# First pass of a graph network kernel: one 384-column scalar-tensor-tensor per dense step in place of three 128-column tensor-scalars in every second step

## Chip, cores and metric

The kernel runs on one core of one Trainium2 chip. The metric is the device time of one execution in microseconds (us), lower is better. Before the change it is 4443.65 us, the median of three runs (4441.05 to 4446.47).

## The reference, cut to what matters

Four graph layers run one after the other on 3125 nodes with 64 features and 50,000 edges (`src`, `dst`, sorted by `dst`). Each layer gathers rows of the source nodes, makes messages and sums them per destination node.

```python
h = jnp.maximum(_layernorm(x), 0.0)
x = x + L0(h, edge_index, edge_attr_16, ...)   # msg = relu(h[src] + edge_attr @ We + be); segment_sum over dst; MLP
x = x + L1(h, edge_weight, src, dst)           # 10 steps: h = 0.9 * segment_sum(h[s] * wn, d) + 0.1 * h0
x = x + L2(h, edge_index, edge_attr_3, ...)    # 3 attention layers over the edges
x = x + L3(h, edge_index, ...)                 # edge convolution, segment_sum over src
```

L1 applies the same weighted adjacency matrix ten times. The kernel therefore builds that matrix once, dense, while it computes L0, and L1 is then a series of plain matrix products.

## The kernel before, in words

Edges are sorted into 416 tiles of 128 (`T`). A pass over the edges handles them in 104 units of `K` = 4 tiles, as 13 iterations (`NB`) of 8 units (`U`). There are five such passes; the change touches the first one, which does L0 and builds the dense matrix at the same time.

Every engine runs its own instruction list, written out by hand, and the lists meet at semaphores. In the first pass one unit is this:

- **GpSimd** (`gather`, L825) issues four indirect DMAs, one per tile, that fetch the rows of the source nodes from the table in HBM into `rows[:, u]`. It may run up to eight units ahead, held by `slots_free`; in each unit it also waits once until the unit before has landed.
- **VectorE** (`turn0` of the vector block) first makes the four one-hots of the *next* unit (`one_hots`: L1169 copies the weights, L1174 makes four 128x128 one-hots). Then `dense_operands` makes the operands of 5 or 6 dense steps (44 in an iteration, 572 in all). Then it copies the transposed payload of the next unit (L1201) and, after `lin_ready`, takes the relu of this unit's messages (L1217).
- **TensorE** transposes the next payload (L1672), makes the messages from payload and gathered rows (it waits for `gathered[u]` there), sums up the unit two before, and then runs the unit's dense steps: three matmuls of 500 columns per step.
- **ScalarE** (`evict`, L1447 and L1449) copies each finished block of the matrix out of PSUM and clears the bank.

A dense step needs two operands. `lhs[:, slot]` holds three weighted one-hots of 128 columns in bf16, one for each of the three bf16 parts into which a float32 weight is split (its largest part, what is left of it, and what is left then). `rhs[:, slot]` is a one-hot of 500 columns (L1158). The operands lie in a ring of `PER2` = 11 slots; `built` says when TensorE has used a slot, `op_ready` when a slot is filled.

Before the change the three weighted one-hots are made in two ways, in turns. An even step uses three tensor-scalars of 128 columns (L1156), each with two per-partition scalars (the edge's row and its weight part from `w_left`). An odd step uses one scalar-tensor-tensor of 384 columns (L1150), whose inputs are the row of column numbers, repeated three times, and the three weight parts from `w_parts`, each repeated 128 times. Both of these inputs lie in SBUF.

Of the kernel before, what the change touches and what calls it, by code (L numbers as in the profile page):

```python
# [25 lines left out]
ALU = mybir.AluOpType  # L26
# [69 lines left out]
def gnn_kernel(nc, x, src, dst, edge_attr_16, edge_attr_3, edge_weight,  # L96
# [3 lines left out]
    with ExitStack() as ctx:  # L100
        def sb(name, shape, dt=F32):
            return ctx.enter_context(nc.sbuf_tensor(name, shape, dt))
# [18 lines left out]
        iota_row_b = sb("iota_row_b", [128, 128], BF16)  # L121
# [72 lines left out]
        def carve(shape, dt=F32):  # L194

            n = 1
            for d in shape[1:]:
                n *= d
            w = -(-n // 2) if dt in (BF16, F16) else n
            assert used[0] + w <= WORDS, (used[0], w)  # L200
            a = arena[0:shape[0], used[0]:used[0] + w]
            used[0] += w
            if dt != F32:
                a = a.bitcast(dt)[:, 0:n]
            if len(shape) > 2:
                names = "abcd"[:len(shape) - 1]
                a = a.rearrange(f"p ({' '.join(names)}) -> p {' '.join(names)}",
                                **{x: d for x, d in zip(names, shape[1:])})
            return a
# [93 lines left out]
        lhs = carve([128, PER2, 3, 128], BF16)  # L303
# [4 lines left out]
        lo_col = carve([128, T])  # L308
        src_blk = carve([128, T])
        src_all = carve([128, T])  # L310
        w_left = carve([128, 3, T])
        w_parts = carve([128, T, 3], BF16)
# [251 lines left out]
        def first_step(u):  # L564

            return u // 2 * PER2 + u % 2 * PER_U[0]
# [275 lines left out]
        def _(v):  # L842
# [299 lines left out]
            def dense_operands(i, u):  # L1142

                first = first_step(u)
                for k in range(PER_U[u % 2]):
                    slot = (first + k) % PER2
                    tile_at, key_at = operand_at["tile", first + k], operand_at["key", first + k]
                    v.wait_ge(built, i * PER_BODY + (first + k + 1))
                    if (first + k) % 2:
                        nc.vector.scalar_tensor_tensor(  # L1150
                            lhs[:, slot], iota_row_b[:].unsqueeze(1).to_broadcast([128, 3, 128]), lo_col[:, bass.ds(tile_at, 1)],
                            w_parts[:, bass.ds(tile_at, 1), :].rearrange("p o c -> p (o c)").unsqueeze(2).to_broadcast([128, 3, 128]),
                            ALU.is_equal, ALU.mult)
                    else:
                        for part in range(3):
                            nc.vector.tensor_scalar(lhs[:, slot, part, :], iota_row_b[:], lo_col[:, bass.ds(tile_at, 1)],  # L1156
                                                    w_left[:, part, bass.ds(tile_at, 1)], ALU.is_equal, ALU.mult)
                    nc.vector.tensor_scalar(rhs[:, slot, :], iota_col_h[:], flat_keys[:, bass.ds(key_at, 1)], None,  # L1158
                                            ALU.is_equal).then_inc(op_ready, 1)

# [42 lines left out]
            def turn0(i, u, before, more):  # L1203
                if u == 0:
                    fetch_operands(i, u)
                if before == 0:
                    one_hots(i, u, pay, C_KEY, True, False)
                    turn_keys(i, u)
                if more:
                    one_hots(i, u + 1, pay, C_KEY, True, False)  # L1210
                dense_operands(i, u)
                if u + 1 < U:
                    fetch_operands(i, u + 1)
                if more:
                    turn_keys(i, u + 1)
                v.wait_ge(lin_ready, i * U + (u + 1))
                nc.vector.tensor_scalar(of(msg, u)[:, :, 0:D], lin(u), 0.0, None, ALU.max).then_inc(msg_ready, 1)  # L1217
# [693 lines left out]
```

## Time and profile before

| | |
|---|---|
| median of 3 runs | 4443.65 us |
| profiled execution | 4435.5 us |
| its span, first to last instruction | 4433.7 us |
| TensorE busy | 3310.6 us (75%) |
| VectorE busy | 2910.4 us (66%) |
| GpSimd busy | 3018.6 us (68%) |
| ScalarE busy | 847.9 us (19%) |
| first pass, first gather to its last matmul | about 657.7 to 1345.8 us |

How to read it: times are microseconds from the start of the span, of one execution taken by the hardware profiler. PE is TensorE, PEld its weight load, DVE is VectorE, ACT is ScalarE, POOL is GpSimd. L1156 is line 1156 of the kernel. Instructions of one engine overlap a little at their ends, so the cost of one among others is read from start to start, not from its own duration.

### The profile page before, as it was taken

What the parts mean: (1) busy time and instruction counts of PE and PEld (TensorE: products, weight loads), DVE (VectorE), ACT (ScalarE), POOL (GpSimd) and SP (SyncE); (2) the same over time, 40 slices, a digit from 0 to 9 for tenths busy, and PEclk for the clock granted to TensorE, in tenths of its full rate; (3) what the DMA queues carried; (4) which work ended last, traced back from release to release, by engine and by line L of the source; (5) the groups of instructions that cost most, each with busy time, mean ns of one, the idle gap of its engine ahead of it and who ended that gap; (6) DMA issues with size and microseconds to landing.
All of it is one profiled execution on the core that took longest, in us unless ns stands there. A gap on an engine that the chain in (4) does not pass through costs nothing.

```text
span 4433.7 us, 80945 instructions
## 1 busy us (share of the span) xinstructions
PE 3310.6 (75%) x20757; PEld 2267.7 (51%) x20758; DVE 2910.4 (66%) x10438; ACT 847.9 (19%) x2207; POOL 3018.6 (68%) x3059
## 2 busy tenths in 40 slices
PE   1269408888887999999687876888858877566666
PEld 1269304554553444443466665666646666445554
DVE  6987319999993111111788887888878888765554
ACT  0000002222221000000122222222212222121121
POOL 2677767788778888840377774777747777467776
PEclk9999999999997999999899996999979999755555
DMA  4310013333458999999222223222232222211112
GB/s 143 108 46 10 17 59 81 88 90 90 92 88 314 356 363 356 363 357 361 80 62 62 61 62 51 63 62 62 62 52 63 62 62 62 33 32 28 28 28 30
DMA packets 295276, 497.76 MB, mean 112 GB/s; under 512 B 165611, under 2 KB 210540, under 8 KB 293674
## 3 DMA queue, kind: packets, MB, share of 16 engines
q1 hardware_dynamic: 120119, 340.02, 21.7%
q0 software_dynamic: 92160, 115.39, 13.6%
q10 hardware_dynamic: 82800, 40.01, 3.1%
q8 instruction: 88, 1.44, 0.1%
q14 instruction: 109, 0.89, 0.1%
HBM read 435.66 MB, written 59.08 MB: 112 GB/s over the span
## 4 chain that ended last, share of the span: by engine, by line
PE 29%; POOL 24%; issue 18%; DMA 16%; DVE 9%; DVEq 1%; SPq 1%; ACT 1%; POOLq 0%; ACTq 0%
PE ps L1565 27%; POOL arena L825 17%; DMA arena<-table,arena 13%; POOL rows_dst L808 7%; DMA rows_dst<-stage,arena 2%; PE ps L1754 1%; DMA arena<-in_edge_attr_dram 1%; DVE arena L1174 1%; DVE arena L1173 1%; DVE arena L1156 1%; DVEq L553 1%; DVE arena L1158 1%; DVE arena L1192 1%; DVE arena L1150 1%; DMA arena<-dense 1%
## 5 line engine op out<-in xcount | busy, mean ns | idle before, releaser
L825 POOL DMA_INDIRECT arena<-table,arena x2080 | 2110.2, 1015 | 1046.5 <-issue 541.3
L1565 PE MATMUL ps<-arena 125*128 (+5 forms) x9976 | 1629.7, 339 | 580.5 <-DVE arena L1192 250.9
L1565 PEld LDWEIGHTS ps<-arena 125*128 125x128 bf16 (+5 forms) x9976 | 1187.8, 206 | 990.8 <-issue 606.5
L1565 PE MATMUL ps<-arena,nodes 125*64 125x500 f32 (+2 forms) x3144 | 651.4, 537 | 34.6 <-DMA arena<-dense 24.1
L1174 DVE TENSOR_SCALAR arena<-iota_row_b,arena 128x128 f32<-128x128 bf16 x2080 | 584.9, 299 | 0.0
L808 POOL DMA_INDIRECT rows_dst<-stage,arena x400 | 401.0, 1002 | 233.0 <-issue 122.2
L779 POOL DMA_INDIRECT rows_src<-stage,stage_at x400 | 479.0, 1197 | 116.4 <-issue 108.4
L1186 DVE TENSOR_TENSOR arena<-ps,arena 128x256 f32<-128x256 f32 x416 | 176.6, 425 | 523.9 <-DMA arena<-table,arena 510.4
L1173 DVE TENSOR_SCALAR arena<-iota_row_b,arena 128x128 bf16<-128x128 bf16 x1664 | 458.4, 277 | 2.7 <-DVE arena L1325 1.1
L1274 DVE TENSOR_TENSOR nodes<-nodes,ps 125x256 f32 (+1 forms) x70 | 27.5, 393 | 609.4 <-PE ps L1754 609.4
L1565 PEld LDWEIGHTS ps<-arena,nodes 125*64 125x64 f32 (+1 forms) x3144 | 244.5, 137 | 351.7 <-issue 320.1
L1803 PE MATMUL ps<-ident_b,arena 128*128 128x128 bf16 x1664 | 197.2, 253 | 127.2 <-DVE arena L1174 125.7
L1565 PE MATMUL ps<-we,arena 128*128 128x128 f32 x1248 | 275.5, 306 | 0.0
L1565 PE MATMUL ps<-wz,arena 96*128 96x128 f32 x1248 | 266.8, 298 | 0.0
L1672 PE MATMUL ps<-ident,arena 128*96 128x128 f32 x416 | 124.4, 299 | 181.6 <-DMA arena<-rows_dst 81.6
L1565 PE MATMUL ps<-arena,wt 96*128 96x128 f32 x1248 | 239.2, 320 | 7.0 <-ACT arena L1472 6.0
L1538 ACT ACTIVATE arena<-arena,ba2c 128x4 f32<-128x4 f32 x312 | 92.8, 297 | 743.7 <-DVE arena L1347 743.7
L1156 DVE TENSOR_SCALAR arena<-iota_row_b,arena 128x128 bf16<-128x128 bf16 x858 | 232.3, 331 | 0.0
L1803 PEld LDWEIGHTS ps<-ident_b,arena 128*128 128x128 bf16 x1664 | 121.0, 112 | 213.0 <-DVE arena L1174 209.2
L1565 PEld LDWEIGHTS ps<-we,arena 128*128 128x128 f32 x1248 | 214.2, 215 | 0.1
L1565 PEld LDWEIGHTS ps<-wz,arena 96*128 96x128 f32 x1248 | 213.9, 214 | 0.0
L1565 PEld LDWEIGHTS ps<-arena,wt 96*128 96x128 f32 x1248 | 186.7, 214 | 26.5 <-ACT arena L1472 18.2
(286 smaller groups left out, 3510.3 us busy)
## 6 DMA issues: line engine op xcount, KB each, us to landing
arena<-dense SPq DMA_DIRECT2D x240, 750.0 KB, 7.5
nodes<-dense SPq DMA_DIRECT2D x60, 750.0 KB, 8.2
dense<-arena ACTq DMA_DIRECT2D x150, 250.0 KB
arena<-table,arena POOLq DMA_INDIRECT x2080
arena<-dense SPq DMA_DIRECT2D x60, 500.0 KB
arena<-rows_dst SPq DMA_DIRECT2D x208, 96.0 KB
arena<-dense SPq DMA_DIRECT2D x6, 2000.0 KB, 21.5
arena<-pair_rows SPq DMA_DIRECT2D x12, 976.6 KB
```

The lines of the kernel that those rows point to most:

```text
L553: _, values = nc.values_load_multi_w_load_instructions(at_, engines=(eng.engine,), min_val=lowest, max_val=highest, skip_runtime_bounds_ch ...
L779: nc.gpsimd.indirect_dma_start(to, bass.IndirectOffsetOnAxis(ap=stage_at[:, h, j:j + 1], axis=0), stage[0:EP, h, j, 0:width], None).then_i ...
L808: nc.gpsimd.indirect_dma_start(rows_all, bass.IndirectOffsetOnAxis(ap=pos_all[:, j0 + j:j0 + j + 1], axis=0), stage[:, h, j, :], None).the ...
L825: nc.gpsimd.indirect_dma_start(rows[:, u, k, 0:width], None, frm, bass.IndirectOffsetOnAxis(ap=p[:, c, j, c_other:c_other + 1].bitcast(I32 ...
L1156: nc.vector.tensor_scalar(lhs[:, slot, part, :], iota_row_b[:], lo_col[:, bass.ds(tile_at, 1)], w_left[:, part, bass.ds(tile_at, 1)], ALU. ...
L1173: nc.vector.tensor_scalar(of(ohb, v_)[:, k, :], iota_row_b[:], key_at, None, ALU.is_equal)
L1174: ins = nc.vector.tensor_scalar(of(oh, v_)[:, k, :], iota_row_b[:], key_at, None, ALU.is_equal)
L1186: nc.vector.tensor_tensor(sums, local_ps[:, :, :, 0], by_two(rows[:, v_ % U, :, at_:at_ + D]), ALU.add).then_inc(add_a, 1)
L1538: nc.scalar.activation(of(att, u), of(logit, u), ACT.Sigmoid, bias=ba2c[:, 0:1]).then_inc(att_ready, 1)
L1565: return nc.tensor.matmul(to, lhsT, rhs, start=start, stop=stop, skip_group_check=True)
L1672: nc.tensor.transpose(to, pay[:, c, j:j + K, :].rearrange("p k c -> p (k c)"), ident[:]).then_inc(tr_ready, 1)
L1803: ins = nc.tensor.transpose(ohT_ps[:, k, :], of(ohb, v_)[:, k, :], ident_b[:])
```

## The change

In the first pass, every dense step now makes its three weighted one-hots by the one scalar-tensor-tensor of 384 columns; no step uses the three tensor-scalars. So 858 tensor-scalars go, and 286 scalar-tensor-tensors come, 572 in all. The number and the order of the dense steps, the one-hots of 500 columns (L1158), the matmuls, the semaphores and everything outside `dense_operands` stay.

```diff
                     v.wait_ge(built, i * PER_BODY + (first + k + 1))
-                    if (first + k) % 2:
-                        nc.vector.scalar_tensor_tensor(
-                            lhs[:, slot], iota_row_b[:].unsqueeze(1).to_broadcast([128, 3, 128]), lo_col[:, bass.ds(tile_at, 1)],
-                            w_parts[:, bass.ds(tile_at, 1), :].rearrange("p o c -> p (o c)").unsqueeze(2).to_broadcast([128, 3, 128]),
-                            ALU.is_equal, ALU.mult)
-                    else:
-                        for part in range(3):
-                            nc.vector.tensor_scalar(lhs[:, slot, part, :], iota_row_b[:], lo_col[:, bass.ds(tile_at, 1)],
-                                                    w_left[:, part, bass.ds(tile_at, 1)], ALU.is_equal, ALU.mult)
+                    nc.vector.scalar_tensor_tensor(
+                        lhs[:, slot], iota_row_b[:].unsqueeze(1).to_broadcast([128, 3, 128]), lo_col[:, bass.ds(tile_at, 1)],
+                        w_parts[:, bass.ds(tile_at, 1), :].rearrange("p o c -> p (o c)").unsqueeze(2).to_broadcast([128, 3, 128]),
+                        ALU.is_equal, ALU.mult)
                     nc.vector.tensor_scalar(rhs[:, slot, :], iota_col_h[:], flat_keys[:, bass.ds(key_at, 1)], None,
                                             ALU.is_equal).then_inc(op_ready, 1)
```

## Rows read from the trace of the kernel before

**Rows 1.** Busy time of each engine (x: instructions) over the first pass.
```profile
657.00:1346.00 689.00, 591.07 (x3069) 342.95 (x3068) 654.19 (x2466) 188.05 (x351) 543.38 (x432) 0.99 0.40 86
```

**Rows 2.** Groups by line in 670 to 1345 us: busy, mean ns, idle before, releaser.
```profile
L825 POOL DMA_INDIRECT arena<-table,arena x407 | 519.6, 1277 | 138.8 <-issue 115.6 <-DMA arena<-table,arena 18.6 <-DMA arena<-rows_dst 4.3
...
L1156 DVE TENSOR_SCALAR arena<-iota_row_b,arena 128x128 bf16<-128x128 bf16 x858 | 232.3, 331 | 0.0
L1158 DVE TENSOR_SCALAR arena<-iota_col_h,arena 128x500 bf16<-128x500 f16 x572 | 198.9, 348 | 0.0
L1150 DVE SCALAR_TENSOR_TENSOR arena<-iota_row_b,arena 128x384 bf16<-128x384 bf16 x286 | 172.5, 603 | 0.0
```

**Rows 3.** Waits in 670 to 1345 us: who waited for whom, total, times, longest.
```profile
PE ps L1565 <- DVE arena L1158: 26.2, 26, 2.6
...
DVE arena L1169 <- issue: 21.1, 8, 3.1
```

**Rows 4.** Timeline of VectorE over one unit of five dense steps: start, length.
```profile
901.83 0.28 DVE L1201 COPY arena<-ps 96x128 f32<-96x128 f32 x1
...
903.22 0.75 DVE L1156 TENSOR_SCALAR arena<-iota_row_b,arena 128x128 bf16<-128x128 bf16 x3
...
903.88 0.34 DVE L1158 TENSOR_SCALAR arena<-iota_col_h,arena 128x500 bf16<-128x500 f16 x1
...
904.14 0.61 DVE L1150 SCALAR_TENSOR_TENSOR arena<-iota_row_b,arena 128x384 bf16<-128x384 bf16 x1
...
904.67 0.34 DVE L1158 TENSOR_SCALAR arena<-iota_col_h,arena 128x500 bf16<-128x500 f16 x1
...
907.58 0.28 DVE L1201 COPY arena<-ps 96x128 f32<-96x128 f32 x1
```

**Rows 5.** GpSimd busy in the gathers of L825: first pass, then a later pass.
```profile
657.00:1328.00 671.00, 528.77 (x416) 0.99 0.41 88
2300.00:2800.00 500.00, 339.75 (x357) 0.89 0.26 60
```

**Rows 6.** Timeline of the gathers of the first pass, with VectorE around one.
```profile
672.13 2.38 POOL L825 DMA_INDIRECT arena<-table,arena  x1 [0.30 <-issue]
...
679.40 1.29 POOL L825 DMA_INDIRECT arena<-table,arena  x1 [0.30 <-issue]
...
681.00 1.55 POOL L825 DMA_INDIRECT arena<-table,arena  x1 [0.31 <-issue]
...
685.36 0.99 POOL L825 DMA_INDIRECT arena<-table,arena  x1 [0.30 <-issue]
...
1027.52 2.00 POOL L825 DMA_INDIRECT arena<-table,arena  x1 [0.31 <-DMA arena<-table,arena]
...
1027.56 0.35 DVE L1158 TENSOR_SCALAR arena<-iota_col_h,arena 128x500 bf16<-128x500 f16 x1
...
1027.82 0.62 DVE L1150 SCALAR_TENSOR_TENSOR arena<-iota_row_b,arena 128x384 bf16<-128x384 bf16 x1
...
1318.13 1.19 POOL L825 DMA_INDIRECT arena<-table,arena  x1 [0.30 <-issue]
...
1320.88 1.80 POOL L825 DMA_INDIRECT arena<-table,arena  x1 [0.31 <-issue]
...
1326.64 1.11 POOL L825 DMA_INDIRECT arena<-table,arena  x1 [0.30 <-issue]
```

**Rows 7.** Timeline: scatters of GpSimd beside back-to-back scalar-tensor-tensors (L940).
```profile
100.64 1.05 POOL L808 DMA_INDIRECT rows_dst<-stage,arena  x1 [0.30 <-issue]
...
101.86 0.35 DVE L940 SCALAR_TENSOR_TENSOR nodes<-arena 125x125 f16<-125x125 f16 x1
...
101.99 1.04 POOL L808 DMA_INDIRECT rows_dst<-stage,arena  x1 [0.30 <-issue]
...
102.12 0.35 DVE L940 SCALAR_TENSOR_TENSOR nodes<-arena 125x125 f16<-125x125 f16 x1
```

**Rows 8.** The relu of the first pass: ns min/median/max, first and last start.
```profile
L1217 DVE TENSOR_SCALAR arena<-ps x104: 401/405/425, 676.2 to 1342.7; 128x256 f32<-128x256 f32 x104
```

## Prediction

> **What bounds the kernel now.** I read the table of time by slices first, then the first pass by engine, by line, by waits, and last the two timelines of VectorE and GpSimd against each other. The change lies wholly in the first pass, from the first gather at about 657 us to the last matmul at about 1346 us. All that follows waits for that end, so what the pass gains or loses is the kernel's gain or loss.
>
> In the pass VectorE is busy 654 of 689 us, TensorE 591 and GpSimd 543 [rows 1]. TensorE waits 26 us for the one-hots of 500 columns and never for a gather; VectorE stands still only at the heads of the iterations, 21 us in 8 waits [rows 3]. So VectorE sets the pace, (1342.7 - 676.2) / 103 = 6.47 us per unit [rows 8].
>
> GpSimd needs a second look, since its share hides how close it is. Its gathers take 1.28 us on average here, and before each there are 0.30 us that wait for nothing shown [rows 2, 6]. 416 of them fill the 671 us from the first to the last: 1.61 us each, 6.45 us per unit [rows 5]. It almost never stands still, and it leads by a few units only: the last gather starts at 1326.64 us, the last relu at 1342.7 us [rows 6, 8]. Two engines thus run at one pace, and GpSimd is the second bound.
>
> What makes it that slow is the core of this case. The same gather takes 339.75 / 357 = 0.95 us in a later pass and 528.77 / 416 = 1.27 us here [rows 5]. Laying the two timelines over each other shows where the 0.32 us come from. I sort the gathers by the VectorE instruction that had started last when the gather was 0.2 us old. For 54 gathers it was one of the three tensor-scalars (L1156): mean 1.01 us, from 0.99 at 685.36 us to 1.11 at 1326.64 us. For 204 it was a scalar-tensor-tensor (L1150): mean 1.47 us. In 82 of these, the first at 679.40 and the last at 1318.13 us, at least 0.41 us of it had passed: 1.22 us. In the other 122, the first at 681.00 and the last at 1320.88 us, it was younger: 1.63 us. Twice it was the one-hot of 500 columns with a scalar-tensor-tensor behind it: 2.38 and 2.00 us [rows 6]. So the scalar-tensor-tensor and the long one-hot hold a gather up, and the three short tensor-scalars are the gaps in which gathers get through.
>
> **The change, part by part.** *VectorE.* Three tensor-scalars cost 903.88 - 903.22 = 0.66 us from start to start, the long one-hot 904.14 - 903.88 = 0.26, the scalar-tensor-tensor 904.67 - 904.14 = 0.53 [rows 4]. An even step goes from 0.92 to 0.79 us, 0.13 less, and 286 of them give 37 us. By busy time it is 232.3 - 172.5 = 60 us [rows 2], but this counts the overlaps of the three twice. If VectorE stayed the bound, the pass would be 37 us shorter: a unit would be 5.5 x 0.79 = 4.35 us of dense steps, 903.22 - 901.83 = 1.39 us of other work [rows 4] and about 0.27 us of iteration head, 6.01 us together.
>
> *TensorE.* Its work is the same, 591 us [rows 1], below either pace; it costs nothing. *Semaphores, DMAs, ScalarE* stay; the evictions only follow the steps.
>
> *GpSimd.* Its base is 0.95 + 0.30 = 1.25 us per gather [rows 5, 6]. What matters is e, the extra per gather while VectorE is in its dense steps. The trace never shows two scalar-tensor-tensors with only a long one-hot between them, so e must be bounded. In a step of 0.79 us, 0.41 us or 52% of the time is a young scalar-tensor-tensor (extra 1.63 - 0.95 = 0.68), 15% an old one (0.27), and 33% the long one-hot, now always with a scalar-tensor-tensor behind it (mean of 1.43 and 1.05: 1.24) [rows 6]. The sum is 0.35 + 0.04 + 0.41 = 0.80 us. This is the lower bound if blocking works as above, for those 1.63 us ended mostly where three tensor-scalars or the copy L1201 came next, and that place is gone. If the 52% lose one more step there, e = 0.80 + 0.52 x 0.79 = 1.21 us. The upper bound is that a blocked gather waits until the dense steps of the unit end, on average half of them: 2.2 us. Below, the bound is no more extra than a place in a fixed rhythm (first rival). I take 1.21, since the two gathers in front of that very sequence [rows 6] both lost again.
>
> A unit needs four gathers, so its time is T = 4.35 + 1.25 x (4 - 4.35 / (1.25 + e)): those that get through during the dense steps, and the rest behind them while VectorE waits for its messages. With e = 1.21, 1.77 get through and T = 7.14 us; GpSimd needs 104 x 7.14 = 743 us where it now needs 671, 72 more. (For the kernel before, with 4.70 us of dense steps and e = 0.5, which is 416 x 0.32 us spread over the 2.6 gathers per unit that meet dense steps, the same formula gives 6.34 against 6.45 measured.) Against that stands the lead: now the pass ends 18 us behind the last gather; with GpSimd as the bound only the landing, the messages and the last dense steps follow. I estimate them at 8 us, since a unit's matmuls take 591 / 104 = 5.7 us [rows 1]. Net: 72 - 10 = 62, rounded to +60 us.
>
> Profiled: 4435.5 + 60 = 4495.5 us. The median stands 8.15 us above the profiled run, so I predict 4443.65 + 60, about 4504 us.
>
> **Rivals.** *1. GpSimd keeps step, and VectorE's 37 us are won (faster).* Elsewhere scatters run beside back-to-back scalar-tensor-tensors of 125 columns, 0.26 us apart, and cost 1.05 us, no more; they start 1.35 us apart, five of those steps [rows 7]. If gathers lock in the same way to two dense steps, 1.58 us, e is 0.33 and VectorE remains the bound: 4443.65 - 37 = 4407 us. For it: the rhythm exists. Against it: there a short accumulator read stands between the instructions, here a long one-hot that blocks by itself. It decides where e is below 0.64 us, at which T is the 6.47 us of now.
>
> *2. The scalar-tensor-tensor doesn't block gathers (faster).* Then the extra belongs to the tensor-scalars, whose removal frees GpSimd, and the 37 us are won as well: 4407 us. The classes of rows 6 speak plainly against it: 1.01 us beside the short tensor-scalars, 1.47 beside the other. The Trainium skill (SBUF — State Buffer, "Who interferes with whom") infers that an instruction with two SBUF inputs takes only the read side of the shared pair, and that making descriptors needs the write side, which would give this outcome, 4407 us; the rows differ.
>
> *3. Lockout (slower by much).* Every gather that is blocked stays so until the unit's dense steps end: e = 2.2, T = 7.78, 809 us for GpSimd, +138 - 10: 4572 us. For it: both gathers of 1027.52 and 672.13 us lost at each change from one to the other, and got through only when short tensor-scalars came. Against it: some gathers get in at the end of a scalar-tensor-tensor.
>
> *4. Balance.* e near 0.7: the gain and the loss meet within 9 us of 4444. With e = 0.80, T = 6.70 and the pass is 16 us longer, 4460 us; that lies inside my forecast.
>
> **How the numbers follow.** A measurement of this kernel can tell a change of about 0.2%, 9 us, from none. My forecast (e from 0.75 to 1.8, 4453 to 4550 us) has 0.52, lockout 0.20, balance 0.06, the first rival 0.16, the second 0.06. So slower 0.72, same 0.06, faster 0.22. The likeliest case gives 4504 us. The range reaches down to 4415, since a rhythm that holds now and then would give part of the 37 us, and up to 4580, just past the lockout's figure; about 0.2 is outside.
>
> **What the profile after would show.** Right: gathers of the first pass well above 1.27 us on average with many over 2 us; VectorE idle before the relu L1217, released by TensorE, which itself waits for gathered rows; VectorE's dense steps still 0.53 and 0.26 us from start to start; GpSimd's idle time unchanged; the later passes the same. Wrong: gathers at 1.3 us or less, VectorE without gaps, and a pass of about 650 us. The weakest step is e: how often a gather gets in where a scalar-tensor-tensor follows the long one-hot is known from two gathers.

## The result, and the profile after

The changed kernel takes 4554.65 us, the median of four runs (4552.12 to 4575.72), against 4443.31 for the kernel before on the same chip: a ratio of 1.0265, 95% interval 1.0249 to 1.0282, so 111 us slower. The prediction was 4504 us, 60 us slower.

The loss lies in the first pass. Its last matmul ends at 1458.5 us where it ended at 1345.8 before, 112.7 us later, and the last turn of layer 1 comes 112.4 us later, so nothing is lost or won from the pass to there. The two profiled executions differ by 117.4 us (4551.1 and 4433.7 us of span); the last 5 us come after 3230 us, among the same instructions, and the record does not explain them. The end of the pass, before and after:

```profile
1345.44 0.38 PE L1565 MATMUL ps<-zeros_b 128*128 128x512 bf16 x1
1458.15 0.38 PE L1560 MATMUL ps<-zeros_b 128*128 128x512 bf16 x1
```

The busy windows, the groups by line, the waits (us in total, times, longest) and the relu's record stand beside [rows 1], [rows 2], [rows 3] and [rows 8]:

```profile
657.00:1346.00 689.00, 546.61 (x2627) 314.00 (x2628) 538.54 (x1645) 164.34 (x308) 570.81 (x363) 0.91 0.33 75
```

```profile
L825 POOL DMA_INDIRECT arena<-table,arena x407 | 642.2, 1578 | 135.8 <-issue 112.8 <-DMA arena<-table,arena 20.8 <-PE ps L1560 2.1
...
L1149 DVE SCALAR_TENSOR_TENSOR arena<-iota_row_b,arena 128x384 bf16<-128x384 bf16 x572 | 348.0, 608 | 0.0
...
L1153 DVE TENSOR_SCALAR arena<-iota_col_h,arena 128x500 bf16<-128x500 f16 x572 | 199.7, 349 | 0.0
```

```profile
DVE arena L1212 <- PE ps L1560: 88.6, 33, 6.2
PE ps L1560 <- DMA arena<-table,arena: 88.4, 27, 6.8
```

```profile
L1212 DVE TENSOR_SCALAR arena<-ps x104: 401/412/430, 675.8 to 1451.8; 128x256 f32<-128x256 f32 x104
```

In the old window of 689 us VectorE falls from 654 busy us to 539 and stands waiting; GpSimd goes from 543 to 571 and has done only 363 of its instructions there, not 432. The mean gather takes 1578 ns where it took 1277. Two waits are new: TensorE for gathered rows (88.4 us), and behind it the relu L1212 for TensorE (88.6 us; 0.8 before). The weight copy L1164 at the head of a unit waits 36.6 us for TensorE too, where it waited 7.3. TensorE's wait for the long one-hots is 23.2 us, hardly less than the 26.2 of [rows 3]. A unit lasts (1451.8 - 675.8) / 103 = 7.53 us instead of 6.47. TensorE now stands still at times, and its granted clock over the window is 0.91 where it was 0.99; this does not set the pace, for the gathers wait 2.1 us for TensorE in the whole pass.

The mean hides what happened. Of the 416 gathers 285 take between 0.94 and 1.25 us, 55 take over 3 us and the longest 5.81; before, none took over 2.4 us [rows 6]. The 68 gathers over 2 us hold 222 of the 258 us that all 416 take beyond 0.945 each (136 before). Here are gathers that get through, one that does not, VectorE beside it, and what then waits:

```profile
1008.08 1.34 POOL L825 DMA_INDIRECT arena<-table,arena  x1 [0.30 <-issue]
1009.73 1.28 POOL L825 DMA_INDIRECT arena<-table,arena  x1 [0.30 <-issue]
1011.31 2.32 POOL L825 DMA_INDIRECT arena<-table,arena  x1 [0.30 <-issue]
1013.94 5.01 POOL L825 DMA_INDIRECT arena<-table,arena  x1 [0.31 <-issue]
1019.26 0.94 POOL L825 DMA_INDIRECT arena<-table,arena  x1 [0.30 <-issue]
...
1014.12 0.61 DVE L1149 SCALAR_TENSOR_TENSOR arena<-iota_row_b,arena 128x384 bf16<-128x384 bf16 x1
1014.64 0.34 DVE L1153 TENSOR_SCALAR arena<-iota_col_h,arena 128x500 bf16<-128x500 f16 x1
1014.90 0.61 DVE L1149 SCALAR_TENSOR_TENSOR arena<-iota_row_b,arena 128x384 bf16<-128x384 bf16 x1
...
1017.79 0.34 DVE L1153 TENSOR_SCALAR arena<-iota_col_h,arena 128x500 bf16<-128x500 f16 x1
1018.31 0.29 DVE L1196 COPY arena<-ps 96x128 f32<-96x128 f32 x1 [0.17 <-PE ps L1667]
1021.31 0.42 DVE L1212 TENSOR_SCALAR arena<-ps 128x256 f32<-128x256 f32 x1 [2.72 <-PE ps L1560]
...
1020.58 0.70 PE L1560 MATMUL ps<-arena,ident 128*128 128x256 f32 x2 [1.87 <-DMA arena<-table,arena]
```

The gather of 1013.94 us begins 0.18 us ahead of five dense steps, 0.79 us each from start to start. It ends at 1018.95, 0.90 us after the place of the last long one-hot is over (1017.79 + 0.26 = 1018.05): as if it had begun only then. All 68 gathers over 2 us end 0.89 to 0.98 us after the dense steps of a unit. Then TensorE waits for its rows and VectorE for TensorE, 2.7 us. The gathers of 1008.08 and 1009.73 met the same two kinds of instruction and lost 0.3 to 0.4 us. I call a gather held when it stays until such a row of instructions is over, or loses several steps.

### The profile page after: what moved, and what is told of

The parts are those of the page before. It is cut to its first block, busy times and chain, and to the rows that moved or that the text cites. A ratio compares the mean times of both kernels' runs of the same rounds, so it can differ in the third digit from the quotient of the medians.

```text
span 4551.1 us, 80087 instructions
## 1 busy us (share of the span) xinstructions
PE 3369.4 (74%) x20757; PEld 2306.1 (51%) x20758; DVE 2875.3 (63%) x9866; ACT 848.0 (19%) x2207; POOL 3144.6 (69%) x3059
## 4 chain that ended last, share of the span: by engine, by line
POOL 34%; issue 21%; PE 21%; DMA 16%; DVE 6%; SPq 1%; POOLq 0%; ACT 0%; DVEq 0%; ACTq 0%
POOL arena L825 27%; PE ps L1560 19%; DMA arena<-table,arena 13%; POOL rows_dst L808 7%; DMA rows_dst<-stage,arena 1%; PE ps L1749 1%; DMA arena<-in_edge_attr_dram 1%; DVE arena L1168 1%; DVE arena L1169 1%; DMA arena<-dense 0%; DVE arena L1187 0%; DVE arena L1337 0%; DVE arena L1183 0%; PE ps L1798 0%; DVE arena L1185 0%
## 5 line engine op out<-in xcount | busy, mean ns | idle before, releaser
L825 POOL DMA_INDIRECT arena<-table,arena x2080 | 2232.4, 1073 | 1037.1 <-issue 558.1
L1560 PE MATMUL ps<-arena 125*128 (+5 forms) x9976 | 1666.2, 344 | 574.9 <-DVE arena L1187 247.7
L1560 PEld LDWEIGHTS ps<-arena 125*128 125x128 bf16 (+5 forms) x9976 | 1215.3, 209 | 1000.6 <-issue 620.7
L1168 DVE TENSOR_SCALAR arena<-iota_row_b,arena 128x128 bf16<-128x128 bf16 x1664 | 457.4, 277 | 1.8 <-DVE arena L1320 0.7
L1149 DVE SCALAR_TENSOR_TENSOR arena<-iota_row_b,arena 128x384 bf16<-128x384 bf16 x572 | 348.0, 608 | 0.0
L1442 ACT COPY arena<-ps 128x500 f32<-128x500 f32 (+1 forms) x175 | 93.1, 532 | 642.9 <-PE ps L1560 614.8
```

What stands on the lines that cost most here:

```text
L825: nc.gpsimd.indirect_dma_start(rows[:, u, k, 0:width], None, frm, bass.IndirectOffsetOnAxis(ap=p[:, c, j, c_other:c_other + 1].bitcast(I32 ...
L1149: nc.vector.scalar_tensor_tensor(lhs[:, slot], iota_row_b[:].unsqueeze(1).to_broadcast([128, 3, 128]), lo_col[:, bass.ds(tile_at, 1)], w_p ...
L1168: nc.vector.tensor_scalar(of(ohb, v_)[:, k, :], iota_row_b[:], key_at, None, ALU.is_equal)
L1442: nc.scalar.copy(ev[:, slot, 0:blocks * LO], ps[:, bank, 0:blocks * LO]).then_inc(ev_ready, 1)
L1560: return nc.tensor.matmul(to, lhsT, rhs, start=start, stop=stop, skip_group_check=True)
```

## The experiments

Twelve kernels ran, in this order of questions. "Before" is the kernel before on the chip of the same batch, 4438 to 4440 us.

**All steps by three tensor-scalars**, the change in the other direction (e1):

```diff
-                    nc.vector.scalar_tensor_tensor(lhs[:, slot], ...)
+                    for part in range(3):
+                        nc.vector.tensor_scalar(lhs[:, slot, part, :], ...)
```

> Every dense step by three tensor-scalars, none by a scalar-tensor-tensor. Lockout theory (scalar-tensor-tensors and long one-hots back to back leave a gather no place to start): no gather over 2 us, mean about 1.05 us, VectorE alone sets the pace at 5.5 x 0.92 + 1.39 + 0.27 = 6.72 us a unit, 26 us over the kernel before: about 4469 us. Rival (gathers are slow for another reason, such as traffic or the long one-hot alone): mean stays near 1.27 us or above; the time is then 4469 us too, or more if the gathers bind.

Measured: 4478.39 us, ratio 1.0091 (1.0073 to 1.0109), 39 us slower. Without a scalar-tensor-tensor gathers take 1.08 us on average, none over 2 us, and GpSimd has time left over: it waits 131 us for payload that comes in by DMA. VectorE is the bound, and the loss is close to the 37 us that 286 steps of 0.13 us cost.

```profile
L825 POOL DMA_INDIRECT arena<-table,arena x407 | 438.8, 1078 | 258.5 <-DMA arena<-rows_dst 131.2 <-issue 110.2 <-DMA arena<-table,arena 17.2
```

**Half of the gathers**, in the changed kernel (e3) and, as the control, in the kernel before (e3b). Both leave out two of the four gathers of every unit in the first pass; those rows stay zero.

```diff
-                            for k in range(K):
+                            for k in range(K // 2 if ep == EP_L0 else K):
```

> The changed kernel, with the rows of two of the four tiles of each unit not fetched in the first pass (zeros stand in their place). Lockout theory: with two gathers a unit GpSimd is no bound even where one of them is locked out, and what is left is VectorE's gain: about 37 us under the kernel before with the same half of the gathers. Rival (the scalar-tensor-tensors slow VectorE or TensorE themselves): no gain, or a loss, against that control.

> Control: the kernel before, with the rows of two of the four tiles of each unit not fetched in the first pass. Both theories: VectorE sets the pace before, so the time stays within 15 us of 4443 us; if gathers were a bound already, it falls by more.

Measured: 4421.55 us (ratio to before 0.9962, 0.995 to 0.9975) and 4436.12 (0.9995, 0.9985 to 1.0005). With GpSimd relieved the change makes the kernel faster than its control, by 15 us. Busy windows, first the change, then the control:

```profile
657.00:1346.00 689.00, 596.08 (x3084) 347.44 (x3084) 617.16 (x1901) 188.98 (x353) 502.85 (x225) 0.98 0.31 79
```

```profile
657.00:1346.00 689.00, 590.02 (x3069) 342.67 (x3068) 653.83 (x2468) 187.91 (x351) 290.78 (x230) 0.99 0.31 76
```

VectorE's work falls by 653.83 - 617.16 = 36.7 us: the 37 us are there. Some 22 of them do not reach the end, since VectorE now stands still more (it waits 15.1 us for TensorE before the weight copy where the control has 2.3, 8.8 against 0.7 before the relu). And the 208 gathers that are left take 2.28 us each, 64 of them over 3 us, against 1.29 in the control. With half its gathers gone GpSimd has room for that; gathers are held here as well.

**How many steps it takes.** Three tensor-scalars in one step of three (e6), where the kernel before has one of two:

```diff
+                    if (first + k) % 3:
                         nc.vector.scalar_tensor_tensor(lhs[:, slot], ...)
+                    else:
+                        for part in range(3):
+                            nc.vector.tensor_scalar(lhs[:, slot, part, :], ...)
```

> The changed kernel with three tensor-scalars in one dense step of three, where the kernel before had one of two and the changed kernel none. Lockout theory (a gather that starts beside a chain of scalar-tensor-tensors and long one-hots stays held until short tensor-scalars come): no gather has to wait past more than two scalar-tensor-tensor steps and the third step lets it go, 0.53 + 0.26 + 0.53 + 0.26 = 1.6 us on top of 0.95, so no gather over 3 us; the mean lies near 1.35 us, VectorE saves about 12 us, and the time is within 4435 to 4475 us. Proportional rival (each scalar-tensor-tensor adds its own share of the loss, the number of steps alone counts): a third of the way from the kernel before to the changed one, 4440 + 37 = about 4480 us, and a third as many gathers over 3 us as in the changed kernel, about 18.

Measured: 4478.31 us, ratio 1.0093 (1.007 to 1.0116). The shape is that of the lockout theory: one gather over 3 us (3.16), 91 over 2 us, mean 1.40. The time is the rival's: waits of one or two steps, 189 us in all against 136 before, cost as much as a third of the change. All steps, one of two, one of three, none by tensor-scalars: 4478, 4440, 4478, 4555 us. The kernel before stands at the lowest of these four, where VectorE's work and the gathers' waits balance.

**Gaps between the steps.** The four short one-hots of the next unit (128 columns, 0.20 us each) lie ahead of the dense steps. Moved between them, one by one (e4), then in two pairs (e9), they cost VectorE nothing more:

```diff
             def dense_operands(i, u, between):
                 for k in range(PER_U[u % 2]):
+                    if k in (1, 3):                  # e4: if k < len(between): between[k]()
+                        for one in between[k - 1:k + 1]:
+                            one()
```

> The changed kernel, with the four short one-hots of the next unit made one at a time ahead of the first four dense steps, not all ahead of the first. VectorE's work is the same. Lockout theory: each short one-hot is a place where a gather can start, so waits end after a step, gathers over 3 us vanish and the time falls well below the 4555 us of the changed kernel, as far as 4407 us if VectorE sets the pace again. Rival (a gather is slowed in proportion to the time that scalar-tensor-tensors and long one-hots take, wherever they stand): 4555 us within 15 us.

> The changed kernel with the next unit's four short one-hots moved between its dense steps, as in the run with one of them between steps, but in two pairs: two ahead of the second dense step and two ahead of the fourth. Gap theory (a gather gets in where the long instructions pause for about 0.4 us or more): waits end at the pairs, no gather over 3 us, mean near 1.3 us, and with VectorE's dense steps 37 us shorter the time comes to 4410 to 4460 us. Rival (a pause of 0.4 us does not do either, it takes the 0.66 us of three tensor-scalars or an idle VectorE): 30 or more gathers over 3 us and 4490 to 4530 us, as with the short one-hots one by one.

Measured: 4513.79 us (ratio 1.0174, 1.0145 to 1.0202) and 4488.09 (1.011, 1.0091 to 1.0129). Gathers over 3 us: 39 and 42. One by one (e4), neither expectation came true: the gathers over 3 us did not vanish, and the time is not within 15 us of 4555. A pair ends some waits and not others; this gather passed one (701.41) and ended behind the dense steps:

```profile
700.66 4.41 POOL L825 DMA_INDIRECT arena<-table,arena  x1 [0.30 <-issue]
...
700.62 0.61 DVE L1152 SCALAR_TENSOR_TENSOR arena<-iota_row_b,arena 128x384 bf16<-128x384 bf16 x1
701.15 0.34 DVE L1156 TENSOR_SCALAR arena<-iota_col_h,arena 128x500 bf16<-128x500 f16 x1
701.41 0.47 DVE L1186 TENSOR_SCALAR arena<-iota_row_b,arena 128x128 f32<-128x128 bf16 x2
701.80 0.61 DVE L1152 SCALAR_TENSOR_TENSOR arena<-iota_row_b,arena 128x384 bf16<-128x384 bf16 x1
...
704.17 0.28 DVE L1215 COPY arena<-ps 96x128 f32<-96x128 f32 x1
```

For the pairs (e9) the rival's count of held gathers came true, with a time just below its range; that this is so because waits that end at a pair are cheaper was not measured by itself.

**Each kind alone.** The changed kernel without its long one-hots (e7), and without its scalar-tensor-tensors (e8). In both TensorE multiplies by zeros, and their times serve for nothing else than to show that the gathers no longer bind.

```diff
-                    nc.vector.tensor_scalar(rhs[:, slot, :], ...)           # e7
-                    nc.vector.scalar_tensor_tensor(lhs[:, slot], ...)       # e8
```

> The changed kernel without its one-hots of 500 columns in the first pass (they are left out, TensorE multiplies by zeros): only scalar-tensor-tensors follow one another in the dense steps. Theory A (the scalar-tensor-tensor alone locks a gather out): gathers over 2 us remain, cut short by the shorter dense run of 5.5 x about 0.5 = 2.9 us, so that the longest is near 3.8 us and the mean of those beside it 1.8 us or more. Theory B (it takes the alternation with the long one-hot): no gather over 2 us, mean 1.3 us or less. VectorE loses 286 x 2 x 0.26 = 150 us of work, so GpSimd's 416 x 1.25 = 520 us or TensorE's 591 us set the pass: the time lies between 4350 and 4420 us by B, and above that by A only if gathers still wait.

> The changed kernel without its scalar-tensor-tensors in the first pass (the weighted one-hots are left out, TensorE multiplies zeros): only the one-hots of 500 columns follow one another, in 0.26 us each. Theory A (the long one-hot does not hold a gather by itself, it only leaves no room between two scalar-tensor-tensors): gathers stay at 0.95 to 1.1 us, none over 2 us. Theory B (both kinds hold it, any unbroken run of long instructions does): gathers that start in the dense run, 5.5 x 0.26 = 1.4 us long, wait for its end, up to 0.95 + 1.4 = 2.4 us, and the mean is near 1.3 us. The time is set by TensorE or GpSimd in both, 4350 to 4400 us.

Measured: 4410.14 and 4407.71 us, one run each, TensorE the bound in both (566 and 568 busy of 630 us). Neither kind alone does it often. First gathers beside six scalar-tensor-tensors in a row, one that gets in (732.04) and one that does not (672.27), then one beside six long one-hots:

```profile
732.04 1.33 POOL L825 DMA_INDIRECT arena<-table,arena  x1 [0.30 <-issue]
733.68 1.82 POOL L825 DMA_INDIRECT arena<-table,arena  x1 [0.30 <-issue]
...
731.42 3.26 DVE L1149 SCALAR_TENSOR_TENSOR arena<-iota_row_b,arena 128x384 bf16<-128x384 bf16 x6
...
672.27 4.26 POOL L825 DMA_INDIRECT arena<-table,arena  x1 [0.30 <-issue]
...
672.45 3.25 DVE L1149 SCALAR_TENSOR_TENSOR arena<-iota_row_b,arena 128x384 bf16<-128x384 bf16 x6
```

```profile
1004.81 0.94 POOL L825 DMA_INDIRECT arena<-table,arena  x1 [0.30 <-DMA arena<-table,arena]
...
1003.98 1.89 DVE L1149 TENSOR_SCALAR arena<-iota_col_h,arena 128x500 bf16<-128x500 f16 x6
```

The gather of 732.04 ends with scalar-tensor-tensors still to come; it lost 0.4 us. 185 gathers began from 0.2 us ahead of such a row to its end: mean 1.31 us, 177 of them under 1.9. The other eight took 2.04 to 4.26 us, and each ended 0.9 us after its row, as that of 672.27 does: they were held like those of the changed kernel. So the scalar-tensor-tensor alone does hold a gather, but 8 of 185, where the two kinds in turn held 68 of 213. Beside long one-hots alone the mean is 0.98 us; one gather of 416 took over 2 us (2.32), and it began beside short ones. My theory for the first of the two runs, that the scalar-tensor-tensor alone locks gathers out, was wrong: nearly always it takes the two kinds in turn. Its rival, theory B, had no gather over 2 us, which these eight contradict.

**The same instructions in another order.** A long one-hot alone holds no gather, so several of them together could be a gap. In twos (e10), in threes (e11), and in twos with the pairs of short one-hots behind (e12):

```diff
+                for at in range(0, len(steps), 2):            # e11: 3
+                    for k in steps[at:at + 2]:
                         nc.vector.scalar_tensor_tensor(lhs[:, slot], ...)
+                    for k in steps[at:at + 2]:
                         nc.vector.tensor_scalar(rhs[:, slot, :], ...).then_inc(op_ready, 1)
+                    if at < 4:                                # e12 alone
+                        for one in between[at:at + 2]:
+                            one()
```

> The changed kernel's own instructions in another order: two scalar-tensor-tensors, then their two one-hots of 500 columns, instead of one and one. VectorE's work is that of the changed kernel (37 us below before). Theory (only the scalar-tensor-tensor holds a gather; the long one-hots are a gap, and a gap of 2 x 0.26 = 0.53 us is long enough to let it in, where 0.26 and 0.39 are not): a gather waits for two scalar-tensor-tensors at most, 1.06 + 0.95 = 2.0 us, none over 2.3 us, mean near 1.25 us, and the time is 4405 to 4440 us. Rival (0.53 us is too short as well, or the long one-hot holds too where it follows the other): 40 or more gathers over 3 us, 4490 to 4560 us.

> The same in threes: three scalar-tensor-tensors, then three one-hots of 500 columns, so that the gap is 0.79 us, longer than that of three tensor-scalars (0.66 us), which let every gather in. Theory (gap length alone): each gap ends every wait, at most 3 x 0.53 + 0.95 = 2.5 us and none over 2.8 us; mean near 1.3 us, since the runs to wait through are longer than in twos; 4415 to 4460 us. Rival (a long one-hot behind a scalar-tensor-tensor holds as well): 40 or more gathers over 3 us, 4490 to 4560 us.

> Two and two, and the next unit's four short one-hots in pairs behind the first and the second such group, so that two gaps of each unit are 0.53 + 0.39 = 0.92 us long. Theory (gap length): as two and two or better, mean gather at or below 1.2 us, none over 2.3 us, VectorE the bound again and 4400 to 4435 us. Rival (long one-hots hold too, and only a pair of short ones, which let 19 waits end and 41 pass, is left as a gap): 25 or more gathers over 3 us and 4470 to 4520 us.

Measured: 4536.86 us (ratio 1.0218, 1.02 to 1.0236), 4527.30 (1.0205, 1.0185 to 1.0224) and 4489.63 (1.0124, 1.0108 to 1.0139), with 57, 51 and 20 gathers over 3 us. These are the rivals' numbers (only the 20 are fewer than the 25 named): the theory that the length of the gap decides has been refuted. This gather of the run in twos passes two gaps of 0.52 us and gets in 0.91 us ahead of its end, at 941.50, when the last dense step is over:

```profile
936.59 5.82 POOL L825 DMA_INDIRECT arena<-table,arena  x1 [0.30 <-issue]
...
936.77 1.14 DVE L1152 SCALAR_TENSOR_TENSOR arena<-iota_row_b,arena 128x384 bf16<-128x384 bf16 x2
937.83 0.61 DVE L1159 TENSOR_SCALAR arena<-iota_col_h,arena 128x500 bf16<-128x500 f16 x2
938.35 1.14 DVE L1152 SCALAR_TENSOR_TENSOR arena<-iota_row_b,arena 128x384 bf16<-128x384 bf16 x2
...
941.50 0.29 DVE L1202 COPY arena<-ps 96x128 f32<-96x128 f32 x1
```

**Kind or size.** The last run makes the long one-hot, from the same operands into the same place, by three tensor-scalars of 168, 168 and 164 columns (e13):

```diff
-                    nc.vector.tensor_scalar(rhs[:, slot, :], iota_col_h[:], ...).then_inc(op_ready, 1)
+                    for piece in (slice(0, 168), slice(168, 336), slice(336, CW)):
+                        ins = nc.vector.tensor_scalar(rhs[:, slot, piece], iota_col_h[:, piece], ...)
+                    ins.then_inc(op_ready, 1)
```

> The changed kernel with each one-hot of 500 columns made by three tensor-scalars of 168, 168 and 164 columns, so that the same data is written in about 0.66 us instead of 0.26. Theory (what lets a held gather in is a row of short instructions: three long one-hots in a row, 0.79 us, let none in, three tensor-scalars of 128 columns, 0.66 us, always): each row of pieces ends the wait, no gather over 2.2 us, mean 1.05 to 1.2 us. Rival (it is the operands: a one-hot of column numbers in half precision holds whatever its length): 40 or more gathers over 3 us, up to 0.95 + 5.5 x 1.2 = 7.5 us, mean above 1.5. VectorE's unit grows by 5.5 x 0.4 = 2.2 us, 6.01 + 2.2 = 8.2 where the kernel before has 6.47, so the time is about 4440 + 103 x 1.74 = 4620 us by the theory and some 4700 us by the rival.

Measured: 4533.64 us in one run. Two gathers took over 2.2 us (2.35 and 2.90), where the theory had none; all others under 2. Of those that wait, all but one get in at the next pieces, after one scalar-tensor-tensor.

```profile
900.81 1.79 POOL L825 DMA_INDIRECT arena<-table,arena  x1 [0.30 <-issue]
...
900.62 0.60 DVE L1154 TENSOR_SCALAR arena<-iota_col_h,arena 128x168 bf16<-128x168 f16 x3
901.13 0.61 DVE L1149 SCALAR_TENSOR_TENSOR arena<-iota_row_b,arena 128x384 bf16<-128x384 bf16 x1
901.66 0.60 DVE L1154 TENSOR_SCALAR arena<-iota_col_h,arena 128x168 bf16<-128x168 f16 x3
```

The mean is 1.33 us, above the 1.05 to 1.2 expected, since now many gathers wait for one scalar-tensor-tensor (157 of 416 took 1.7 to 1.9 us). VectorE is the bound and the time 4440 + 103 x (7.4 - 6.47) = 4536 us by its unit of 5.5 x 1.05 + 1.66 = 7.4 us; I had taken the pieces at 0.66 us where they take 0.51 to 0.52, hence 4620. With 5.5 x 0.26 = 1.4 us more work for VectorE per unit it is still not slower than the changed kernel's 4555 us: no gather is held for long.

**What lets a held gather in.** From the timelines of these runs I counted rows of instructions in the dense steps that began 0.4 us or more after a gather had. They stand behind a scalar-tensor-tensor, or, in e4, e9, before and e6, behind the long one-hot that follows one. A row ended the wait if the gather was over 0.75 to 1.15 us after its start, and was passed if the gather was still there 0.75 us after its end. Where exactly these limits are set moves single counts by up to four.

| Row on VectorE, us from start to start | Kernel | Waits ended | Passed |
|---|---|---|---|
| one one-hot of 500 columns, 0.26 | changed | 13 | 262 |
| two of them, 0.52 | e10 | 3 | 107 |
| three of them, 0.79 | e11 | 0 | 67 |
| one short one-hot in f32, 0.20 | e4 | 3 | 79 |
| two short ones, 0.39 | e9 | 28 | 41 |
| three pieces of 168, 168, 164 columns, 0.52 | e13 | 187 | 1 |
| three tensor-scalars of 128 columns, 0.66 | before, e6 | 167 | 0 |

(Three rows of e6, of each of which the trace holds a single record, are not in the table. The expectation of e12 gives 19 waits ended for e9; by this rule it is 28.) Two long one-hots and three pieces take the same 0.52 us; the two let 3 of 110 in, the pieces 187 of 188. So the time between two scalar-tensor-tensors does not decide, and neither do the operands, which the pieces share with the long one-hot. Three long one-hots against three pieces, 0 of 67 against 187 of 188, show that the size of the single instruction does. The number in a row seems to count as well (one short one-hot let 3 of 82 in, two 28 of 69); two pieces or one were not tried.

## Why the prediction was right, and where it was right by luck

*Direction and place: right.* GpSimd was the second bound as read from [rows 5, 6]; it became the first bound, TensorE waits for gathers and the relu for TensorE, as foretold. The instructions kept their 0.53 and 0.26 us. Half the gathers turned the sign, and steps without scalar-tensor-tensors freed GpSimd.

*VectorE's 37 us: right, and worth nothing here.* 36.7 us of busy time went in the pair with half the gathers; a unit that no gather disturbs takes 6.11 and 5.32 us in the changed kernel (six and five steps), 6.54 and 5.63 before.

*The extra per gather, e: right by its mean, by luck, and wrong in its make-up.* 213 gathers met the dense steps (204 young or old scalar-tensor-tensors, 9 long one-hots) and lost 257.5 us: 1.21 each, the value taken from bounds of 0.80 and 2.2. But no typical gather loses 1.21. 40 beside an old scalar-tensor-tensor take 1.16 us, most others under 1.6, and the 55 over 3 us carry 204.5 us of it. The step that named the cause, one further step lost where the three tensor-scalars had been, fits at most 13 gathers of about 2.3 us, and these too end where the dense steps do. The third rival's mechanism, held to the end of the dense steps, happened to about one gather in three of those that met them (68 of 213). That the mean over held and free ones comes out at 1.21 is luck, and the 4555 us lie nearer to that rival's 4572 than to the 4504 that I gave.

*The formula for T: the step that failed.* It lets 4.35 / (1.25 + e) = 1.77 gathers per unit meet the dense steps; 213 / 104 = 2.05 did. A held gather runs its 0.9 us after the dense steps are over (1018.05 to 1018.95), and may begin ahead of them, so that 213 gathers fill 213 x (0.945 + 1.21 + 0.30) = 523 us while the dense steps last 104 x 4.35 = 452. The sum then goes: forecast 743 us for GpSimd, of it 104 x 1.77 x 1.21 = 223 of extra; measured extra 258, so +35; GpSimd's idle time beyond 0.30 us per gather, which the formula leaves out and which had shown in its 6.34 against 6.45 us for the kernel before, +12. Together 790; from 657.74 to 1447.28 us the gathers take 789.5. Before they took 670.0 (657.71 to 1327.75), so that is +119.5, not +72. The lead shrinks from 18.1 to 11.2 us (1458.5 - 1447.3), -6.8 where I took -10. 119.5 - 6.8 = 112.7 us, by which the pass is longer; the medians differ by 111.

*The rivals.* The first (gathers fall in step with the dense steps) does occur, as in the gathers of 1008.08 and 1009.73, but a held one follows. The second, that scalar-tensor-tensors do not hold gathers, is refuted as a forecast: with no scalar-tensor-tensor (e1) the gathers are free and the kernel is 39 us slower by VectorE's work, with one in every step it is 111 us slower. (In the third, T is 7.77 by the formula, not 7.78; nothing hangs on it.) The Trainium skill (SBUF — State Buffer, "Who interferes with whom") says that VectorE and GpSimd share a pair of ports and the loser is blocked for the whole instruction of the other, and infers that an instruction with two inputs in SBUF leaves the writing of descriptors alone. With either kind by itself the trace nearly agrees with the first (means of 1.31 and 0.98 us, eight held); with both in turn it differs, 5.01 us past ten instructions. It differs from the second in both cases, but a gather also takes its row numbers from SBUF, so that inference may not have been meant for it.

*Open.* Why the two kinds in turn shut a gather out so often, when each alone nearly always lets it in, is not shown. Nor was it tried at how many columns a row of three stops letting it in, nor is it shown why one gather is held and another is not. The start alone does not tell: of 39 that began 0.15 to 0.20 us ahead of a scalar-tensor-tensor in the changed kernel 23 were held and 16 not, while of the 37 that began 0.24 to 0.30 us after one none was.

## What to carry to other kernels

When a fast engine's instructions are merged into longer ones, ask who used the seams: here three short tensor-scalars in every second step were the only places in the dense steps where a gather on GpSimd surely got in, and the net loss was three times the 37 us that VectorE saved. A mean over classes seen before the change is a poor price for a sequence that never stood there; look at whether the loss can last as long as the sequence, and count too what the held engine still has to do behind it. If an engine's gathers sit close behind the bound, test a VectorE saving with the gathers halved before trusting it.

## What the runs showed of the hardware

- Beside scalar-tensor-tensors and long one-hots in turn a gather on GpSimd takes 1.2 to 1.6 us or else up to 5.81 us, and a held one ends about 0.9 us after the row does (0.89 to 0.98 in 68 cases). Five or six scalar-tensor-tensors in a row held 8 of 185 gathers, long one-hots alone none of the 93 that began beside them.
- Three tensor-scalars of 128 to 168 columns let a waiting gather in (354 of 355); three of 500 columns, 0.79 us, never (0 of 67); two of 128 columns in f32 in 28 of 69 cases.
- Of five orders of the changed kernel's own instructions (e4, e9 to e12) none beat the kernel before; the fastest took 4488 us.
